# A stream of 64 tiles: one written order for all engines becomes a table with an order for each engine

## The chip, the cores and the metric

The kernel runs on one NeuronCore of a Trainium2 chip. The metric is the device time of one execution in microseconds (us). The engines are TensorE (PE: matrix products and transposes into PSUM), VectorE (DVE), ScalarE (ACT), GpSimd (POOL) and SyncE (SP, which issues the DMAs). Each runs its own instructions strictly in the order in which they are written, and they meet only in semaphores.

## The reference

Four residual blocks over x of shape (4, 512, 128), each on a layer norm of x without affine part:

```python
x = x + attn_a(layernorm(x))     # 16 heads of 8, full softmax
x = x + ffn(layernorm(x))        # two layers: local attention + MLP
x = x + attn_b(layernorm(x))     # linear attention, 16 heads of 8
x = x + ffn(layernorm(x))        # the same two layers, same weights
# one layer of ffn, on h = shift_token(x)
q, k, v = split(h @ wqkv)                    # 8 heads of 64
q, k = rotary_xpos(l2norm(q) * qs, l2norm(k) * ks)
x = x + softmax(mask(8 * q @ k.T)) @ v @ wo  # windows of 64, one back
h = layernorm(shift_token(x)) * lg + lb
a, g = split(h @ w1 + b1)
x = x + (a * gelu(g)) @ w2 + b2
```

All is float32. The change lies in the part that runs both calls of ffn and attn_b between them.

## The kernel before

Attention a comes first, in blocks of its own. Then `stream` runs the rest as one pipeline. A tile is 128 tokens; four tiles are a group (one sequence in one layer); 4 sequences x 2 layers x 2 calls make 16 groups and 64 tiles. `stream_plan` writes one list of (stage, number) pairs, 72 steps long. In step s tile s is projected (`project`: 9 products) and its q and k are rotated on DVE (`rope`: products with cos and sin, L1391 and L1395, then the sums of squares L1402 and the clip L1406); POOL adds the two halves (L971) and multiplies by the reciprocal norms (L976) in the stage `scale`, for which ACT makes the norms (L1279, L1283). Tile s-1 is transposed (`turn`, L1052), copied by ACT (L1258, L1262), scored (`scores`: masks L1065, products L1078) and softened (`soften`: maxima on DVE L1423, exponents on ACT L1272). Tile s-2's exponents are transposed (`turn_p`, L1089) in two halves, of which ACT copies the first (L1290) and DVE the second (L1415), and multiplied with v (`sums`, L1100, then L1430 and L1434 on DVE). Tile s-3's result is transposed (`turn_o`, L1112).

Once in four steps the work of a whole group comes in. I call the steps by it:

| step mod 4 | name here | group work |
|---|---|---|
| 3 | norm step | layer norm before the MLP: `center` (L1153), square (L1311), `var` (L1158), L1317, L1320, L1448, L1452 |
| 0 | w1 step | `w1`: 12 passes of PE (L1165), gelu on ACT between two table loads (L1323, L1328, L1331), three products on DVE (L1468) |
| 1 | w2 step | `w2`: 6 passes (L1173), then L1485 and L1489, or L1478 in the last layer |
| 2 | wo step | `wo`: 8 passes (L1138), Y (L1440), copies on POOL (L991, L993) |

In steps 26 to 41 attention b of each sequence is spread over four further stages: centre, variance and latent (wo step), keys (norm step: L1189, L1509, L1516), context, tokens and features (w1 step: L1196, L1206, L1533 to L1540, L1213), projection, centre and variance (w2 step: L1218, L1546, L1153, L1158, L1457, L1460).

Every engine walks the same list and picks the stages in which it has work, so a stage's place in the list is its place on every engine. PSUM has 8 banks, handed out in turn in PE's order; a product waits until the user of the bank eight places earlier has freed it (`take`).

Of the kernel before, what the change touches and what calls it, by code (L numbers as in the profile page):

```python
# [14 lines left out]
P = 128  # L15
# [701 lines left out]
def stream_plan():  # L717

    plan, norms, number = [], [], {}

    def tile(k, *stages):
        if 0 <= k < TOTAL:
            plan.extend((stage, k) for stage in stages)

    def group(k, *stages):

        if k % TILES == TILES - 1 and 0 <= k < TOTAL:  # L730
# [24 lines left out]
    def var(k, use):
        if k % TILES == TILES - 1 and 0 <= k < TOTAL:
            m = k // TILES
            if use == "mlp" or last_layer(m) and not last_call(m):
                plan.append(("var", number[use, m if use == "mlp" else m % SEQS]))

    for step in range(TOTAL + 8):
        tile(step, "project", "rope")
        group(step - 6, "w2")
        center(step - 7, "b")
        tile(step - 3, "turn_o")
        center(step - 4, "mlp")
        group(step - 5, "w1")
        sequence(step - 9, "context")
        sequence(step - 10, "project_b")
        tile(step - 1, "turn")  # L770
        group(step - 3, "wo")
# [18 lines left out]
    return plan, norms, number  # L790


def stream(nc, a, g, out):

    psum, X, Y, eps, cst, cstb = g.psum, g.X, g.Y, g.eps, g.cst, g.cstb
    plan, norms, number = stream_plan()

    order = []
    for stage, i in plan:
        if stage == "project":  # L800
            order += [("q", i), ("k", i), ("v", i)]
# [37 lines left out]
    with ExitStack() as ctx:  # L839
# [76 lines left out]
        with block:  # L916
            @block.sync
            def _(sp):
# [5 lines left out]
                for stage, k in plan:  # L924
                    if stage == "turn":
# [19 lines left out]
            def _(pool):  # L945
# [21 lines left out]
                for stage, i in plan:  # L967
# [41 lines left out]
                    elif stage == "var" and norms[i][0] == "y":  # L1009
                        n = norms[i][1]  # L1010
                        pool.wait_ge(s("ln_used"), i + 1)
                        low_part(n, "again_shifted", 2 * n)

            @block.tensor
            def _(pe):
# [68 lines left out]
                def turn_p(k):  # L1084
                    for u in (2 * k, 2 * k + 1):
                        pe.wait_ge(s("exped"), u + 1)
                        dst = take("turn_p", u)
                        for c in range(PAIRS):
                            last = nc.tensor.transpose(dst[:, P * c:P * c + P], PW[:, u % 4, c, :], g.ident)  # L1089
                        last.then_inc(s("turned_p"), 1)  # L1090
# [27 lines left out]
                for stage, i in plan:  # L1118
# [6 lines left out]
                    elif stage == "turn_p":  # L1125
                        turn_p(i)
# [14 lines left out]
                    elif stage == "center":  # L1141
                        use, j = norms[i]
# [426 lines left out]
```

## Time and profile before

| what | us |
|---|---|
| time, median of 3 runs (1241.07 to 1248.66) | 1245.42 |
| time of the profiled execution | 1247.89 |
| its span, first to last instruction | 1246.1 |
| PE busy, of the span | 998.1 (80%) |
| DVE busy | 798.1 (64%) |
| ACT busy | 703.9 (56%) |
| POOL busy | 390.8 (31%) |
| mean granted TensorE clock, share of full speed | 0.922 |

The profiled execution's own time is 1.8 us above its span and 2.5 us above the median of the runs. The stream begins some 390 us into the span. Busy time of PE is modelled at the ends of products, so the text goes by the starts of the rows. A group in the forms below is named by its line in the kernel, its engine, and what it writes from what it reads.

### The profile page before, as it was taken

Reading aid. Unit: us, or ns where it says so; the run is one execution under the profiler, and the core shown is the slowest. Engines: PE = TensorE matmul, PEld = TensorE weight load, DVE = VectorE, ACT = ScalarE, POOL = GpSimd, SP = SyncE. Lnnn points to the kernel's source line nnn. Section 1 sums busy time; section 2 is a strip of 40 time slices with the busy share of each in tenths; the row PEclk is TensorE's granted clock in tenths of the full one; section 3 lists DMA queues with packets and bytes.
Section 4 is the critical chain, followed back from the end, with each engine's and each line's share of the span. In section 5 each row is a group of like instructions: output and inputs, shape, how many; then the busy total and the mean of one; then the engine's idle time right before and its main releaser. Section 6 shows DMA issues by size and latency. Waiting matters only on the chain.

```text
span 1246.1 us, 22091 instructions
## 1 busy us (share of the span) xinstructions
PE 998.1 (80%) x8250; PEld 602.5 (48%) x8272; DVE 798.1 (64%) x1381; ACT 703.9 (56%) x1500; POOL 390.8 (31%) x251
## 2 busy tenths in 40 slices
PE   4079986069985788889889898989898898898886
PEld 2023333013323666666556665656565665666652
DVE  4088825058825668678677685867677786676751
ACT  3037763017773567557566565656666576576662
POOL 5000015000003553534444434342434435344330
PEclk9589998569997799999899999999999999999998
DMA  2950001950002211011010010000001010101100
GB/s 65 129 100 9 1 1 38 113 70 2 1 2 51 57 23 22 19 22 23 18 24 14 18 23 18 14 18 14 18 14 23 19 23 19 23 14 35 31 10 17
DMA packets 38268, 36.01 MB, mean 29 GB/s; under 512 B 11478, under 2 KB 30224, under 8 KB 38160
## 3 DMA queue, kind: packets, MB, share of 16 engines
q1 hardware_dynamic: 34708, 31.46, 13.8%
q10 hardware_dynamic: 3456, 3.15, 1.2%
q8 instruction: 67, 1.10, 0.4%
q14 instruction: 37, 0.30, 0.1%
HBM read 15.41 MB, written 4.21 MB: 16 GB/s over the span
## 4 chain that ended last, share of the span: by engine, by line
PE 28%; DVE 13%; POOL 11%; ACT 9%; issue 6%; POOLq 0%; DVEq 0%; ACTq 0%
PE psum L1165 6%; PE psum L1138 5%; POOL f_A L976 4%; POOL f_A L971 4%; ACT f_PW L1272 4%; PE psum L1052 3%; PE psum L1078 2%; PE psum L1089 2%; DVE f_A L1391 2%; DVE f_BS L1395 2%; POOL f_HL L963 2%; DVE f_NM L1423 2%; DVE f_SS L1402 2%; PE psum L1100 2%; PE psum L1158 1%
## 5 line engine op out<-in xcount | busy, mean ns | idle before, releaser
L1272 ACT ACTIVATE f_PW<-psum,f_NM 128x128 f32<-128x128 f32 x512 | 139.3, 383 | 127.9 <-DVE f_NM L1423 127.9
L500 DVE TENSOR_REDUCE a_M<-psum 128x1 f32<-128x512 f32 x256 | 160.2, 684 | 67.5 <-remote 38.7
L976 POOL TENSOR_TENSOR f_A<-f_A,f_RN 128x1024 f32<-128x1024 f32 x64 | 121.7, 1902 | 252.3 <-ACT f_RN L1283 250.0
L971 POOL TENSOR_TENSOR f_A<-f_A,f_BS 128x1024 f32<-128x1024 f32 x64 | 151.6, 2368 | 46.5 <-DVE f_BS L1395 45.0
L430 PE MATMUL psum<-a_KS,a_QS 128*128 128x512 bf16 x238 | 96.7, 413 | 79.7 <-DMA a_KS<-minus_ones 75.9
L547 ACT ACTIVATE a_PT<-psum 128x1024 f32<-128x1024 f32 x128 | 126.4, 1018 | 56.5 <-PE psum L452 56.1
L1391 DVE TENSOR_TENSOR f_A<-psum,cos 128x512 f32<-128x512 f32 x128 | 87.9, 686 | 93.5 <-ACT f_SQ L1240 93.5
L1052 PE MATMUL psum<-const,f_A 128*128 128x128 f32 x512 | 76.8, 299 | 49.6 <-POOL f_A L976 49.6
L452 PE MATMUL psum<-a_QS,a_KS 128*128 128x512 bf16 x252 | 94.5, 390 | 14.6 <-DMA a_QS<-a_MROW 10.4
L1423 DVE TENSOR_REDUCE f_NM<-psum 128x4 f32<-128x512 f32 x128 | 82.3, 685 | 36.4 <-PE psum L1078 36.4
L1042 PE MATMUL psum<-f_wqkv_h,f_HH 128*128 128x512 f32 x192 | 86.7, 451 | 23.0 <-DVE Y L1460 13.1
L430 PEld LDWEIGHTS psum<-a_KS,a_QS 128*128 128x128 bf16 x256 | 25.4, 100 | 159.0 <-DMA a_KS<-minus_ones 75.5
L1052 PEld LDWEIGHTS psum<-const,f_A 128*128 128x128 f32 x512 | 64.8, 154 | 73.3 <-POOL f_A L976 62.9
L1165 PE MATMUL psum<-f_mid,f_w 128*128 128x512 f32 (+1 forms) x192 | 89.7, 619 | 2.7 <-DVE f_mid L1452 2.7
L1100 PE MATMUL psum<-f_VS,f_PT 128*64 128x65 f32 x1024 | 73.8, 225 | 17.9 <-DVE f_mid L1448 12.1
L1395 DVE TENSOR_TENSOR f_BS<-psum,sin 128x512 f32<-128x512 f32 x128 | 87.2, 681 | 0.0
L1100 PEld LDWEIGHTS psum<-f_VS,f_PT 128*64 128x64 f32 x1024 | 65.5, 138 | 30.0 <-issue 30.0
L1402 DVE TENSOR_REDUCE f_SS<-f_SQ 128x16 f32<-128x1024 f32 x64 | 77.4, 1210 | 0.0
L1044 PE MATMUL psum<-f_wqkv_h,f_HL 128*128 128x512 f32 x192 | 76.9, 401 | 0.0
L1043 PE MATMUL psum<-f_wqkv_l,f_HH 128*128 128x512 f32 x192 | 76.9, 400 | 0.0
L1100 PE MATMUL psum<-f_V,f_PT 128*64 128x65 f32 x1024 | 74.1, 226 | 0.0
L1240 ACT ACTIVATE f_SQ<-psum 128x512 f32<-128x512 f32 x128 | 68.5, 585 | 7.6 <-PE psum L1044 7.6
(173 smaller groups left out, 1966.5 us busy)
## 6 DMA issues: line engine op xcount, KB each, us to landing
f_VS<-f_V SPq DMA_DIRECT2D x112, 130.0 KB, 2.3
parts<-a_PRT ACTq DMA_DIRECT2D x24, 128.0 KB, 2.4
a_QS<-parts SPq DMA_DIRECT2D x8, 256.0 KB
a_KS<-parts SPq DMA_DIRECT2D x8, 256.0 KB
a_QS<-parts SPq DMA_DIRECT2D x4, 384.0 KB
a_KS<-parts SPq DMA_DIRECT2D x4, 384.0 KB
raw<-L_ffn_wqkv_dram SPq DMA_DIRECT2D x2, 768.0 KB, 7.0
a_XT<-L_attn_a_x_dram SPq DMA_DIRECT2D x4, 256.0 KB, 4.0
```

The source lines that it names most:

```text
L430: nc.tensor.matmul(psum[:, take("tile", 8 * unit + k), :], QS[:, n, h + k // 4, P * qt:P * qt + P], KS[:, n, h + k // 4, :], start=True, s ...
L500: nc.vector.tensor_reduce(M[:, u % 4, k // 4, k % 4:k % 4 + 1], psum[:, bank("tile", i), :], AX_X, ALU.max)\
L547: nc.scalar.activation(PT[:, head % 8, 2 * (half % 2):2 * (half % 2) + 2, :], psum[:, SLOT[i % 2][0]:SLOT[i % 2][1] + 1, :], ACT.Exp, scal ...
L971: nc.gpsimd.tensor_tensor(A[:, k % 2, :, :], A[:, k % 2, :, :], BS[:, k % 2, :, :], ALU.add)\
L976: nc.gpsimd.tensor_tensor(x, x, RN[:, k % 2, :, None].to_broadcast([P, 2 * HW, DW]), ALU.mult)\
L1052: last = nc.tensor.transpose(dst[:, P * c:P * c + P], A[:, k % 2, w, P * c:P * c + P], g.ident)
L1100: last = nc.tensor.matmul(dst[WIN * w:WIN * w + WIN, c, :], PT[:, u % 4, c, WIN * w:WIN * w + WIN], values[:, k % 4, 2 * c + j, :], start= ...
L1165: nc.tensor.matmul(take(kind, 3 * i + blk)[0:w, :], w1[:, layer, first + lo:first + lo + w], mid[:, :], start=True, stop=True).then_inc(s( ...
L1272: last = nc.scalar.activation(PW[:, u % 4, c, :], psum[:, bank("scores", u), P * c:P * c + P], ACT.Exp, bias=NM[:, u % 4, c:c + 1])
L1391: nc.vector.tensor_tensor(A[:, k % 2, w, :].rearrange("p (h d) -> p h d", d=DW), x.rearrange("p (h d) -> p h d", d=DW), g.cos[:, layer, t, ...
L1395: nc.vector.tensor_tensor(BS[:, k % 2, w, :].rearrange("p (h s d) -> p h s d", s=2, d=DW // 2), x.rearrange("p (h s d) -> p h s d", s=2, d ...
L1423: nc.vector.tensor_reduce(NM[:, u % 4, :], psum[:, bank("scores", u), :].rearrange("p (c x) -> p c x", c=PAIRS), AX_X, ALU.max, negate=Tru ...
```

## The change

`stream_plan` goes. A table `STEP` gives for each engine its own list of stages with their lags, and `engine_plan(engine)` unrolls one engine's list. Banks are still handed out in PE's order. Some stages are cut in two: `project` on ACT into `squares` and `values`, `scale` on ACT becomes `norm`, `turn_p` on PE into two halves, `w1` on DVE into two blocks and the last one (`w1_last`), `center` and `var` into one for each of the three norms. No instruction is added or taken away, and no buffer changes.

```diff
-def stream_plan():
...
-    for step in range(TOTAL + 8):
-        tile(step, "project", "rope")
-        group(step - 6, "w2")
-        center(step - 7, "b")
-        tile(step - 3, "turn_o")
-        center(step - 4, "mlp")
-        group(step - 5, "w1")
-        sequence(step - 9, "context")
-        sequence(step - 10, "project_b")
-        tile(step - 1, "turn")
-        group(step - 3, "wo")
-        tile(step - 2, "turn_p")
-        var(step - 4, "mlp")
-        var(step - 7, "b")
-        center(step - 10, "y")
-        sequence(step - 8, "keys_b")
-        sequence(step - 9, "tokens_b")
...
-        tile(step - 1, "scores")
-        tile(step - 1, "soften")
-        tile(step, "scale")
-        tile(step - 2, "sums")
-        var(step - 10, "y")
-        sequence(step - 7, "latent")
-        sequence(step - 9, "features_b")
+STEP = {
+    "PE": [("project", 0, of_tile), ("turn", 1, of_tile), ("context", 9, of_sequence), ("project_b", 10, of_sequence),
+           ("turn_o", 3, of_tile), ("w1", 5, of_group), ("turn_p", 2, of_tile),
...
+           ("keys_b", 8, of_sequence), ("tokens_b", 9, of_sequence), ("scores", 1, of_tile),
...
+           ("turn_p_2", 2, of_tile), ("latent", 7, of_sequence), ("features_b", 9, of_sequence),
+           ("w2", 6, of_group), ("wo", 3, of_group), ("sums", 2, of_tile), ("store", 6, of_end)],
...
+def engine_plan(engine):
+    plan = []
     for step in range(TOTAL + 8):
...
+        for stage, lag, whose in STEP[engine]:
+            k = step - lag
+            if 0 <= k < TOTAL and whose(k) is not None:
+                if stage == "lead" and not 1 <= k < SEQS or stage == "split" and k >= 3:
+                    continue
+                plan.append((stage, whose(k)))
+    return plan
...
-                for stage, i in plan:
-                    if stage == "project":
+                for stage, i in engine_plan("ACT"):
+                    if stage == "squares":
```

On ACT, from step 50 into step 51 (f_QT and f_KT are the copies of the transposed q and k, f_PW the exponents, f_LN and f_RN the norms, f_SQ the squares, f_V the values), there stood from one copy of q on:

```order
709 L1258 ACTIVATE f_QT<-psum 128x512
710 L1262 ACTIVATE f_KT<-psum 128x4x128
711 L1290 ACTIVATE f_PT<-psum 128x512
712 L1272 ACTIVATE f_PW<-psum,f_NM 128x128 x8
713 L1279 ACTIVATE f_LN<-f_SS 128x16
714 L1283 ACTIVATE f_RN<-f_LN 128x16
715 L1240 ACTIVATE f_SQ<-psum 128x512 x2
716 L1249 ACTIVATE f_V<-psum 128x8x64
```

and stands now:

```order
707 L1257 ACTIVATE f_QT<-psum 128x512
708 L1261 ACTIVATE f_KT<-psum 128x4x128
709 L1248 ACTIVATE f_V<-psum 128x8x64
710 L1298 ACTIVATE f_OT<-psum 128x4x128
711 L1289 ACTIVATE f_PT<-psum 128x512
712 L1278 ACTIVATE f_LN<-f_SS 128x16
713 L1282 ACTIVATE f_RN<-f_LN 128x16
714 L1271 ACTIVATE f_PW<-psum,f_NM 128x128 x8
```

The norms of a tile have moved from behind the exponents of the tile before it to ahead of them; the copies of values stand behind those of q and k.

On DVE, in step 49, a w2 step (f_SS is the clip, f_HH and Y the sum of the MLP, f_PT the copy of the second half of the transposed exponents, f_NM the maxima), there stood:

```order
823 L1406 TENSOR_TENSOR f_SS<-f_SS,tiny 128x16
824 L1485 SCALAR_TENSOR_TENSOR f_HH<-psum,f_vecs,Y 64x512
825 L1485 SCALAR_TENSOR_TENSOR f_HH<-psum,f_vecs,Y 64x511
826 L1489 SCALAR_TENSOR_TENSOR Y<-psum,f_vecs,Y 128x512
827 L1415 COPY f_PT<-psum 128x512
828 L1423 TENSOR_REDUCE f_NM<-psum 128x4 x2
829 L1430 RECIPROCAL f_RD<-psum 128x4
```

and stands now:

```order
823 L1407 TENSOR_TENSOR f_SS<-f_SS,tiny 128x16
824 L1424 TENSOR_REDUCE f_NM<-psum 128x4 x2
825 L1416 COPY f_PT<-psum 128x512
826 L1488 SCALAR_TENSOR_TENSOR f_HH<-psum,f_vecs,Y 64x512
827 L1488 SCALAR_TENSOR_TENSOR f_HH<-psum,f_vecs,Y 64x511
828 L1492 SCALAR_TENSOR_TENSOR Y<-psum,f_vecs,Y 128x512
829 L1431 RECIPROCAL f_RD<-psum 128x4
```

The maxima have moved up, and the copy f_PT stands behind them instead of ahead.

On PE, in step 42 (the first wo step behind attention b), behind the projections, there stood `turn_o`, `turn`, `wo`:

```order
1890 L1112 MATMUL psum<-const,f_ON 128x128 x4
1891 L1052 MATMUL psum<-const,f_A 128x128 x8
1892 L1138 MATMUL psum<-f_OT,f_wo 128x512 x4
```

and behind those `turn_p` and the scores. Now there stands:

```order
1930 L1047 MATMUL psum<-const,f_A 128x128 x8
1931 L1106 MATMUL psum<-const,f_ON 128x128 x4
1932 L1083 MATMUL psum<-const,f_PW 128x128 x4
1933 L1060 MATMUL psum<-constb 64x512 x4
1934 L1073 MATMUL psum<-f_KT,f_QT 64x128 x16
1935 L1083 MATMUL psum<-const,f_PW 128x128 x4
1936 L1134 MATMUL psum<-f_OT,f_wo 128x512 x4
1937 L1094 MATMUL psum<-f_VS,f_PT 64x65
```

`wo` has moved behind the scores, and the second half of `turn_p` too, just ahead of the sums that read its copy.

## Rows read from the trace of the kernel before

**Rows 1.** Page, part 5: the squares (busy, mean ns of one)

```profile
L1240 ACT ACTIVATE f_SQ<-psum 128x512 f32<-128x512 f32 x128 | 68.5, 585 | 7.6 <-PE psum L1044 7.6
```

**Rows 2.** Waits: engine and line, whom for: us in total, times, longest

```profile
POOL f_A L976 <- ACT f_RN L1283: 250.0, 48, 8.3
```

**Rows 3.** Timeline of steps 53 and 54: start, length, instruction, [idle before]

```profile
1072.93 0.18 DVE L1406 TENSOR_TENSOR f_SS<-f_SS,tiny 128x16 f32<-128x16 f32 x1
...
1076.57 2.17 ACT L1272 ACTIVATE f_PW<-psum,f_NM 128x128 f32<-128x128 f32 x8 [2.71 <-DVE f_NM L1423]
...
1080.45 1.90 POOL L976 TENSOR_TENSOR f_A<-f_A,f_RN 128x1024 f32<-128x1024 f32 x1
...
1082.41 1.97 PE L1052 MATMUL psum<-const,f_A 128*128 128x128 f32 x8 [3.02 <-POOL f_A L976]
```

**Rows 4.** Windows: stretch, length, busy time by engine, granted clock (PEclk)

```profile
1082.30:1083.80 1.50, 1.39 (x7) 1.40 (x8) 1.17 (x2) 0.24 (x1) 0.05 (x1) 0.50 0.41 93
...
1052.90:1056.00 3.10, 3.06 (x41) 2.68 (x42) 2.64 (x7) 2.05 (x9) 0.00 (x0) 1.00 0.00 0
```

**Rows 5.** Timeline of PE, steps 51 to 55

```profile
1043.44 0.50 PE L1042 MATMUL psum<-f_wqkv_h,f_HH 128*128 128x512 f32 x1
...
1048.72 1.04 PE L1089 MATMUL psum<-const,f_PW 128*128 128x128 f32 x8
1049.60 1.02 PE L1158 MATMUL psum<-f_ln_squared,const 128*128 128x512 f32 x2
...
1050.79 1.04 PE L1078 MATMUL psum<-f_KT,f_QT 64*64 64x128 f32 x32
...
1054.02 0.50 PE L1042 MATMUL psum<-f_wqkv_h,f_HH 128*128 128x512 f32 x1
...
1056.65 3.60 PE L1165 MATMUL psum<-f_mid,f_w 128*128 128x512 f32 x8
...
1066.39 0.50 PE L1042 MATMUL psum<-f_wqkv_h,f_HH 128*128 128x512 f32 x1
...
1076.61 0.50 PE L1042 MATMUL psum<-f_wqkv_h,f_HH 128*128 128x512 f32 x1
...
1090.36 0.27 PE L1100 MATMUL psum<-f_VS,f_PT 128*64 128x65 f32 x1
...
1091.45 0.50 PE L1042 MATMUL psum<-f_wqkv_h,f_HH 128*128 128x512 f32 x1
...
1093.63 0.60 PE L1112 MATMUL psum<-const,f_ON 128*128 128x128 f32 x4
```

**Rows 6.** Timeline of DVE, step 55

```profile
1094.36 0.69 DVE L1391 TENSOR_TENSOR f_A<-psum,cos 128x512 f32<-128x512 f32 x1 [1.45 <-ACT f_SQ L1240]
...
1098.00 1.32 DVE L1406 TENSOR_TENSOR f_SS<-f_SS,tiny 128x16 f32<-128x16 f32 x1
...
1099.24 0.68 DVE L1415 COPY f_PT<-psum 128x512 f32<-128x512 f32 x1
```

**Rows 7.** Line L1402, once for each tile: the whole line, then tiles 11, 26, 42

```profile
L1402 DVE TENSOR_REDUCE f_SS<-f_SQ x64: 1207/1209/1214, 401.4 to 1190.5; 128x16 f32<-128x1024 f32 x64
...
519.87 1.21 DVE L1402 TENSOR_REDUCE f_SS<-f_SQ 128x16 f32<-128x1024 f32 x1
699.01 1.21 DVE L1402 TENSOR_REDUCE f_SS<-f_SQ 128x16 f32<-128x1024 f32 x1
940.46 1.21 DVE L1402 TENSOR_REDUCE f_SS<-f_SQ 128x16 f32<-128x1024 f32 x1
```

**Rows 8.** Timeline of DVE in attention b: keys, maxima; tokens

```profile
842.85 0.75 DVE L1509 TENSOR_SCALAR f_NEGK<-psum 128x256 f32<-128x256 f32 x2
...
844.94 1.28 DVE L1423 TENSOR_REDUCE f_NM<-psum 128x4 f32<-128x512 f32 x2
...
856.78 0.19 DVE L1533 TENSOR_SCALAR f_DEN<-psum 128x32 f32<-128x32 f32 x1 [0.27 <-PE psum L1206]
...
858.35 0.42 DVE L1540 TENSOR_TENSOR f_OB<-psum,f_DEN 128x256 f32<-128x256 f32 x1
```

More of the change, by code:

```diff
@@ L803, in stream @@
             order += [("turned_q", i), ("turned_k", i)]
-        elif stage in ("turn_p", "scores", "sums", "keys_b", "tokens_b"):
+        elif stage in ("scores", "sums", "keys_b", "tokens_b"):
             order += [(stage, 2 * i), (stage, 2 * i + 1)]
+        elif stage in ("turn_p", "turn_p_2"):
+            order += [("turn_p", 2 * i + (stage == "turn_p_2"))]
         elif stage == "w1":
@@ L809, in stream @@
             order += [("latent", i), ("query_b", i)]
-        elif stage in ("turn_o", "wo", "center", "var", "w2", "context", "features_b", "project_b", "store"):
+        elif stage[:7] == "center_":
+            order += [("center", number[stage[7:], i])]
+        elif stage[:4] == "var_":
+            order += [("var", number[stage[4:], i])]
+        elif stage in ("turn_o", "wo", "w2", "context", "features_b", "project_b", "store"):
             order += [(stage, i)]
@@ L923, in _ @@
                 sp.wait_ge(s("zeroed"), 3)
-                for stage, k in plan:
-                    if stage == "turn":
+                for stage, k in engine_plan("SP"):
+                    if stage == "values":
                         sp.wait_ge(s("v_copied"), k + 1)
@@ L965, in low_part @@
                         pool.wait_ge(s(done), before + half + 1)
-                for stage, i in plan:
+                for stage, i in engine_plan("POOL"):
                     if stage == "scale":
@@ L1082, in scores, with turn_p @@
                     last.then_inc(s("scores"), 1)
[L1084 to L1090, printed above, removed]
+                def turn_p(u):
+                    pe.wait_ge(s("exped"), u + 1)
+                    dst = take("turn_p", u)
+                    for c in range(PAIRS):
+                        last = nc.tensor.transpose(dst[:, P * c:P * c + P], PW[:, u % 4, c, :], g.ident)
+                    last.then_inc(s("turned_p"), 1)
                 def sums(k):
@@ L1381, in _ @@
                                             ALU.subtract).then_inc(s("lead_shifted"), 1)
-                for stage, i in plan:
+                for stage, i in engine_plan("DVE"):
                     if stage == "rope":
@@ L1409, in _ @@
                         lead(i)
[L1410 removed]
+                    elif stage == "turn_p_2":
                         u = 2 * i + 1
@@ L1441, in _ @@
                           .then_inc(s("y_mid"), 1)
-                    elif stage == "var":
-                        use, j = norms[i]
-                        x = psum[:, bank("center", i), :]
-                        dve.wait_ge(s("ln_recip"), i + 1)
+                    elif stage[:4] == "var_":
+                        use, j = stage[4:], i
+                        at_norm = number[use, j]
+                        x = psum[:, bank("center", at_norm), :]
+                        dve.wait_ge(s("ln_recip"), at_norm + 1)
                         if use == "mlp":
```

131 lines of the change are left out of this document (66 added, 65 removed).

## The prediction, as it stands on record

> **What bounds the kernel now.** I read the page first, then the waits, then the timeline of one group of the stream, engine by engine. Of all engines PE is busiest, but its busy time does not say where it waits. The waits do: the largest in the stream is POOL's before the multiplication by the norms, 250 us in 48 times, and ACT is what it waits for [rows 2]. Rows 3 show the case. The clip of tile 53 is done at 1073.1, so its norms could follow. But ACT's list puts them behind the exponents of tile 52, which end at 1078.7, since those wait for maxima. POOL then still adds the halves and multiplies until 1082.35, and PE, idle for 3.02 us, transposes. Behind the wait PE ran at half its clock (1.2 instead of 2.4 GHz) [rows 4]. So the chain scores, maxima, exponents, norms, multiplication, transposition, copies, scores runs through every step.
>
> How much of a group is waiting I get from PE's own work [rows 5]. A pass over 512 columns takes 0.43 (8 passes of L1165 in 3.60, ends overlapping); projection 2.18 (1091.45 to 1093.63); `turn` or a whole `turn_p` 0.88 (1048.72 to 1049.60), `turn_o` half of it, 0.43; the norm's product with the masks 1.19 (1049.60 to 1050.79), of which I give the product 0.95; masks and scores so 0.24 + 1.0; sums 1.09 (1090.36 to 1091.45). A step without group work is 2.18 + 0.88 + 0.43 + 0.88 + 1.25 + 1.09 = 6.7. With two norm products the norm step is 8.6, with 12 passes the w1 step 11.9, with 6 the w2 step 9.3, with 8 the wo step 10.2: 40.0 a group. The starts of the projections (lines L1042) give 10.6, 12.4, 10.2 and 14.8 for the four, 48.0 in all [rows 5]. So 8 us of each group are waits and low clock, 4.6 of them in the wo step (3.0 wait, 1.6 clock).
>
> **The change, part by part.** No instruction comes or goes, so what counts is what each waits for in the new lists. I set P = 0 where PE starts a step's projection.
>
> *Norms ahead of exponents.* q is projected at P + 1.0, squared 0.6 later [rows 1], so DVE's rotation starts at P + 1.7. From there to the end of the clip it takes 4.96 (1094.36 to 1099.32) [rows 6]: P + 6.7. The two norms on ACT lie within the 1.7 between the exponents' end and the multiplication in rows 3; I take 0.6, as one of the squares, and bound them by 0 and 1.7. POOL multiplies in 1.9 [rows 3]. That gives P + 9.3, with 1.7 P + 10.4. The transposition comes at 2.2 in the next step, so it waits no more if a step has 7.1 or more (8.2 by the upper bound). The 3.02 in the wo step and the smaller waits of this kind go.
>
> *Copy of the second half behind the maxima.* This is the new wait. PE's sums of the second half need DVE's copy, DVE's copy comes behind the maxima, and these behind the clip. In a short step: clip done 6.7, maxima 1.28 [rows 8], copy 0.68 [rows 6], half of the sums 0.55: the next projection cannot start before P + 1.0 + 0.7 + 4.96 + 1.28 + 0.68 + 0.55 and some 0.15 between them = 9.3. This ring replaces the old chain. The norm step becomes 9.3 (work 8.6), the w2 step 9.4 (work 9.3), the wo step 10.5: its work is 10.2, and it starts with DVE 1 us late from Y of the w2 step, so the copy comes at 9.9, just as PE gets to it. In the w1 step the 12 passes lie ahead of the scores: they end at 2.18 + 0.88 + 0.43 + 5.16 + 0.43 + 1.25 + 0.1 = 10.4, and maxima, copy and half the sums bring 10.4 + 1.28 + 0.68 + 0.55 + 0.15 = 13.05, which is 0.65 slower than the 12.4 of before. ACT's gelu, its second table load and its copy of the first half run under the scores there; if the copy were late by its whole length it would cost 0.7 a group. The group: 9.3 + 13.05 + 9.4 + 10.5 = 42.3 against 48.0.
>
> *The clip itself* took 0.18 at 1072.93 and 1.32 at 1098.00; the second time POOL's addition was running and both ended together [rows 3, 6]. In the new order the addition starts 1.1 ahead of it in almost every step, so I take 1.32 always. With 0.18 the ring would be 8.2 and the norm step PE's 8.6. The Trainium skill ("SBUF — State Buffer", section "Who interferes with whom") has a rule for it: a DVE instruction with two SBUF inputs and a GpSimd one that reads SBUF exclude each other, and the one issued first holds the port to its end. By that rule, and the row at 1098.00 agrees, the clip always pays here; without it the group would be about 41.6 and the time some 9 us less.
>
> *Scores inside the layer norm.* In the norm step the scores separate `center` and `var`. ACT's square ends under the scores, so `var` waits for nothing, and the bank wait of the sums for the layer norm's output goes. All of this is inside the 9.3 above.
>
> *Products moved past copies and SP.* SP's moves of v are issued on `values`, still a step and more ahead of the sums. ACT copies v 1.2 later than before. Nothing waits for that. If it did, it would cost at most 1.2 in a step.
>
> *Attention b, 16 steps.* Here the new lists lose. In the w1 step, `features` (PE) needs DVE's tokens, which now stand behind the copy. Context and tokens add 1.0 and 1.0 to PE (I take eight 144-column passes each, from 0.43 for 512), so the scores end at 12.5; maxima and copy bring 14.6, and the tokens take 2.0 (856.78 to 858.77) [rows 8]: 16.7. PE idles from 12.9. Then features 0.4, and the third block of `w1` on DVE frees the sums' bank: 17.4 + 1.1 = 18.5. In the w2 step `center` for y stands ahead of the scores and needs x, which DVE writes behind the clip: 6.7 + 0.75 = 7.5, PE idle 2.7; then center 0.95, scores 1.25, var 0.95, half `turn_p` 0.43, w2 2.6, sums 1.1: 14.8. In the wo step `latent` stands ahead of `wo` and needs Y, for which DVE goes through clip, maxima, copy and Y (6.7 + 1.3 + 0.7 + 0.7 = 9.4, PE idle 2); latent's four passes at most 1.7, wo 3.4, sums 1.1: 15.7. In the norm step the keys put 2.1 between clip and maxima (842.85 to 844.94) [rows 8]: 9.3 + 2.1 = 11.4. Together 60.4 a cycle. Before, 16 such steps took 940.46 - 699.01 = 241.5, 60.4 a cycle [rows 7]. So nothing is won. The waits of 3.6, 2.7 and 2.0 can each let the clock fall at 1.6 a time; bounds 0 and 4.8 a cycle, and I take 1.0.
>
> **The sum**, by stretches between the squares' sums of tiles [rows 7]. Tiles 0 to 11, 118.5 before: in the first two little can change, and I leave them at 16 (118.5 less nine steps of 11.4, a little under the 11.9 a step of tiles 11 to 26); then five steps of 9.3 (with one norm step), 10.5 twice, 13.05, 9.4 make 90: 106, gain 12. Tiles 11 to 26, 179.1: three groups of 42.3 and three steps of 31.8 in all, 158.7, gain 20. Tiles 26 to 42: 241.5 + 4, loss 4. Tiles 42 to 63, 250.0: five groups and a wo step, 222.0, gain 28. The tail: one short chain less ahead of the last `wo`, gain 3. The gain is 59 to 60 of the profiled execution's 1247.9: 1188. The median of the runs stands 2.5 lower, so I forecast **1185**.
>
> **Rivals.**
>
> 1. *As worked out*, 1172 to 1198. For it: every term is a row's start or length, and the waits it removes recur the same in each group. Chance 0.50.
> 2. *Attention b costs more.* If all three waits let the clock fall and `features` is late by more, 5 to 8 us more a cycle and some of the ramp's gain lost: 1198 to 1222. For it: PE idles longer there than in any plain step of before. Against: the waits themselves, 8.3 a cycle, are already in the terms, and 1.0 of clock with them. Chance 0.19.
> 3. *More is won.* If the clip is not held up or the gaps between stages overlap, the plain groups come near 41 and the wo step to PE's 10.2: 1155 to 1172. Against: the clip at 1098.00. Chance 0.16.
> 4. *DVE sets the pace.* Its list (rotation and clip 5.0, maxima 1.3, copy 0.7, sums 1.2) is 8.2 a step, plus 2.3 for w2 and up to 2.2 for w1. If it carries lateness from one step into the next, plain groups need 45 to 46: 1222 to 1239. Against: it adds to 38 of 42.3 a group. Chance 0.05.
> 5. *Slower: low clock in plain steps.* Many short PE waits, between turn_p and sums, could keep the clock at 1.2 GHz where one long wait let it recover. A fall costs 1.6; some 37 falls in the 64 steps eat the gain of 60, and one in each of the 52 plain or ramp steps gives 1185 + 83 = 1268. Against: behind a wait of 1.1 the window at 1052.9 shows full clock [rows 4], and the new plain waits are 0.7 (norm step) and 1.7 (w1 step), nearly none in the other two. The Trainium skill describes this mechanism ("TensorE: Matmul & The Clock Gate", section "A second HAM failure mode: psum-queue depth-cycling"): frequent small idles between groups of products made the clock swing. By that rule the kernel could be slower; the window of rows 4 speaks against it here. Chance 0.05.
> 6. *No change*: the chain simply reforms at the old length, through a bank that exponents free. Exponents end 3.0 after the maxima start, ahead of the next step's transposition by over 2 us, so I see none. 1239 to 1252, chance 0.02. The rest, 0.03, is below 1155.
>
> **Numbers.** A measurement of this kernel tells a change from none beyond about 0.5%, 6 us. Cases 1 to 4 are faster, 0.93; no change 0.02; slower 0.05. The range 1163 to 1216 takes in case 1, most of 2 and half of 3, some 0.8.
>
> **What would show it.** Right, if in a plain group: POOL's multiplication follows its addition within 0.8 us; PE no longer waits for it; the projections start 9.3, 13, 9.4 and 10.5 apart; PE's only waits are in the middle of the sums, for the copy by DVE; and if in attention b PE waits 3 to 4 us for DVE's tokens ahead of `features`. Wrong, if the clip is short in most steps (then faster), if the granted clock in plain groups falls under 0.95, or if the attention b cycle takes over 65 us.

## The result, and the profile after

| | before | after |
|---|---|---|
| median of 4 runs each, us | 1247.04 | 1192.95 |
| lowest to highest | 1241.07 to 1249.16 | 1191.47 to 1193.12 |
| span of the profiled execution | 1246.1 | 1191.1 |
| mean granted clock | 0.922 | 0.925 |

The ratio is 0.9582, 95% interval 0.9532 to 0.9631: 54 us faster. 1185 was forecast, with 1163 to 1216 as the range.

Where POOL waited before its multiplication [rows 2], this is what its waits say now (engine and line, whom for: total, times, longest):

```profile
POOL f_A L966 <- DVE f_BS L1396: 219.2, 58, 10.4
...
POOL f_A L971 <- ACT f_RN L1282: 107.0, 59, 5.4
```

The multiplication (now L971) waits 107 us in place of 250. The 219 in front of the addition L966 is idle time that costs nothing: POOL stands ready before DVE has written its halves. PE's own waits, the same view:

```profile
PE psum L1094 <- DVE f_PT L1416: 18.0, 26, 3.3
...
PE psum L1210 <- DVE f_OB L1543: 13.3, 4, 3.4
...
PE psum L1149 <- DVE X L1549: 7.9, 4, 2.4
PE psum L1175 <- DVE Y L1462: 6.9, 4, 1.7
PE psum L1047 <- POOL f_A L971: 5.4, 4, 3.4
PE psum L1094 <- DVE f_mid L1450: 5.1, 4, 1.3
```

PE waits for the multiplication (L1047, before L1052) only 4 times, all of them in the first steps of the stream; before it was 49.6 us in 27 times. New is the middle of the sums (L1094, behind DVE's copy). The other places that occur four times each lie in attention b: `features` (L1210) and `latent` (L1175), both new, `center` for y (L1149), and the sums that wait for the bank of f_mid. The waits for X and for f_mid were there before too (6.5 us in 4 times, 12.1 us in 11); of those for f_mid the ones in plain groups are gone.

The timeline of a plain group (steps 45 to 48) answers to [rows 3, 5, 6]:

```profile
944.30 0.50 PE L1037 MATMUL psum<-f_wqkv_h,f_HH 128*128 128x512 f32 x1
...
953.78 0.50 PE L1037 MATMUL psum<-f_wqkv_h,f_HH 128*128 128x512 f32 x1
...
958.75 2.36 POOL L966 TENSOR_TENSOR f_A<-f_A,f_BS 128x1024 f32<-128x1024 f32 x1 [1.10 <-DVE f_BS L1396]
...
959.77 1.37 DVE L1407 TENSOR_TENSOR f_SS<-f_SS,tiny 128x16 f32<-128x16 f32 x1
...
961.42 0.21 ACT L1282 ACTIVATE f_RN<-f_LN 128x16 f32<-128x16 f32 x1
...
961.71 1.90 POOL L971 TENSOR_TENSOR f_A<-f_A,f_RN 128x1024 f32<-128x1024 f32 x1 [0.61 <-ACT f_RN L1282]
...
961.78 2.18 ACT L1271 ACTIVATE f_PW<-psum,f_NM 128x128 f32<-128x128 f32 x8
...
964.12 0.50 PE L1037 MATMUL psum<-f_wqkv_h,f_HH 128*128 128x512 f32 x1
...
972.72 0.27 PE L1094 MATMUL psum<-f_VS,f_PT 128*64 128x65 f32 x1 [0.33 <-DVE f_PT L1416]
...
973.33 0.50 PE L1037 MATMUL psum<-f_wqkv_h,f_HH 128*128 128x512 f32 x1
...
985.80 0.27 PE L1094 MATMUL psum<-f_VS,f_PT 128*64 128x65 f32 x1 [0.81 <-DVE f_PT L1416]
986.42 0.50 PE L1037 MATMUL psum<-f_wqkv_h,f_HH 128*128 128x512 f32 x1
```

Clip, norms, multiplication now follow each other, and the exponents begin beside the multiplication, no longer ahead of it. The projections start 9.48 (w2 step), 10.34 (wo step), 9.21 (norm step) and 13.09 (w1 step) apart, 42.12 in all. The windows over this group and over tiles 42 to 63 show the clock at 1.00 (length, busy time of PE, PEld, DVE, ACT and POOL, granted clock, DMA share, GB/s):

```profile
944.30:986.45 42.15, 41.01 (x423) 28.65 (x419) 37.39 (x62) 31.58 (x78) 20.68 (x13) 1.00 0.11 24
...
916.64:1137.40 220.76, 215.21 (x2180) 150.49 (x2173) 191.27 (x317) 164.28 (x398) 109.58 (x71) 1.00 0.12 26
```

It is 1.00 over tiles 11 to 26 too, and 0.95 over tiles 26 to 42. The squares' sums, L1403, one for each tile, answer to [rows 7] (the whole line, then tiles 11, 26, 42):

```profile
L1403 DVE TENSOR_REDUCE f_SS<-f_SQ x64: 1206/1208/1210, 398.6 to 1137.4; 128x16 f32<-128x1024 f32 x64
...
503.31 1.21 DVE L1403 TENSOR_REDUCE f_SS<-f_SQ 128x16 f32<-128x1024 f32 x1
661.46 1.21 DVE L1403 TENSOR_REDUCE f_SS<-f_SQ 128x16 f32<-128x1024 f32 x1
916.64 1.21 DVE L1403 TENSOR_REDUCE f_SS<-f_SQ 128x16 f32<-128x1024 f32 x1
```

| stretch, us | before | forecast | after |
|---|---|---|---|
| tiles 0 to 11 | 118.5 | 106 | 104.7 |
| tiles 11 to 26 | 179.1 | 158.7 | 158.2 |
| tiles 26 to 42, attention b | 241.5 | 245.5 | 255.2 |
| tiles 42 to 63 | 250.0 | 222.0 | 220.7 |
| last tile to the end | 55.6 | 3 less | 53.8 |

Three stretches came within 1.3 us. Attention b lost 13.7 instead of 4. These 9.7 us, less the 3.1 more that the other three won, and 1.2 less at the end, are nearly the whole distance from 1185 to 1193.

### The profile page after: what moved, and what is told of

Read it like the earlier page. It is cut to its first block, busy times and chain, and to the rows that moved or that the text cites. A ratio compares the mean times of both kernels' runs of the same rounds, so it can differ in the third digit from the quotient of the medians.

```text
span 1191.1 us, 22117 instructions
## 1 busy us (share of the span) xinstructions
PE 1000.9 (84%) x8272; PEld 595.0 (50%) x8272; DVE 827.9 (70%) x1381; ACT 718.4 (60%) x1500; POOL 391.0 (33%) x251
## 4 chain that ended last, share of the span: by engine, by line
PE 48%; DVE 11%; issue 3%; ACT 3%; POOL 2%; DVEq 0%; POOLq 0%
PE psum L1162 7%; PE psum L1094 5%; PE psum L1134 5%; PE psum L1037 4%; PE psum L1073 4%; PE psum L1170 3%; PE psum L1047 3%; PE psum L1039 3%; PE psum L1038 3%; PE psum L1083 3%; DVE f_NM L1424 2%; DVE f_A L1392 2%; PE psum L1106 2%; DVE f_BS L1396 2%; DVE f_SS L1403 2%
## 5 line engine op out<-in xcount | busy, mean ns | idle before, releaser
L966 POOL TENSOR_TENSOR f_A<-f_A,f_BS 128x1024 f32<-128x1024 f32 x64 | 151.0, 2359 | 219.5 <-DVE f_BS L1396 219.2
L430 PE MATMUL psum<-a_KS,a_QS 128*128 128x512 bf16 x256 | 104.9, 419 | 76.1 <-DMA a_KS<-minus_ones 73.8
L971 POOL TENSOR_TENSOR f_A<-f_A,f_RN 128x1024 f32<-128x1024 f32 x64 | 121.9, 1904 | 107.7 <-ACT f_RN L1282 107.0
L1271 ACT ACTIVATE f_PW<-psum,f_NM 128x128 f32<-128x128 f32 x512 | 138.9, 382 | 14.0 <-DVE f_NM L1424 10.9
L1237 ACT ACTIVATE f_SQ<-psum 128x512 f32<-128x512 f32 x128 | 75.9, 609 | 84.2 <-PE psum L1039 79.6
L1094 PE MATMUL psum<-f_VS,f_PT 128*64 128x65 f32 x1024 | 81.8, 230 | 23.5 <-DVE f_PT L1416 18.0
L1094 PEld LDWEIGHTS psum<-f_VS,f_PT 128*64 128x64 f32 x1024 | 68.8, 141 | 56.4 <-issue 29.3
L1094 PE MATMUL psum<-f_V,f_PT 128*64 128x65 f32 x1024 | 82.1, 230 | 0.0
L1407 DVE TENSOR_TENSOR f_SS<-f_SS,tiny 128x16 f32<-128x16 f32 x64 | 80.3, 1255 | 2.2
L1083 PE MATMUL psum<-const,f_PW 128*128 128x128 f32 x512 | 79.0, 277 | 0.0
L1403 DVE TENSOR_REDUCE f_SS<-f_SQ 128x16 f32<-128x1024 f32 x64 | 77.3, 1208 | 0.0
```

The source lines that it names most:

```text
L430: nc.tensor.matmul(psum[:, take("tile", 8 * unit + k), :], QS[:, n, h + k // 4, P * qt:P * qt + P], KS[:, n, h + k // 4, :], start=True, s ...
L966: nc.gpsimd.tensor_tensor(A[:, k % 2, :, :], A[:, k % 2, :, :], BS[:, k % 2, :, :], ALU.add)\
L971: nc.gpsimd.tensor_tensor(x, x, RN[:, k % 2, :, None].to_broadcast([P, 2 * HW, DW]), ALU.mult)\
L1094: last = nc.tensor.matmul(dst[WIN * w:WIN * w + WIN, c, :], PT[:, u % 4, c, WIN * w:WIN * w + WIN], values[:, k % 4, 2 * c + j, :], start= ...
L1271: last = nc.scalar.activation(PW[:, u % 4, c, :], psum[:, bank("scores", u), P * c:P * c + P], ACT.Exp, bias=NM[:, u % 4, c:c + 1])
```

## The experiments

All kernels change only the lists of stages, except where the clip is named. The stretches in the table are measured between the squares' sums on DVE, from one profiled execution each; the 390 us or so ahead of the stream differ by up to 6 us from run to run, so a stretch says more than a median. The profiled executions lie within 5 us of their medians, but that of x17_wo_both lies 7.9 above. A single step comes out otherwise by the squares' sums than by the starts of PE's projections, where an order moves DVE against PE; the text says which it uses. The groups of after, x1, x2 and x4 are alike to 0.6 us; those of before differ among themselves, 46.6 to 49.6, and so do those of x5 and x9. Each ratio is taken against the runs of the kernel before that were made beside it (medians 1245.3 to 1247.3). The four columns behind the ratio are: tiles 0 to 11; a plain group; an attention b cycle (a quarter of tiles 26 to 42); tiles 42 to 63.

| kernel | median | ratio [95%] | 0-11 | group | cycle | 42-63 |
|---|---|---|---|---|---|---|
| before | 1247.04 | 1 | 118.5 | 48.0 | 60.4 | 250.0 |
| after | 1192.95 | 0.9582 [0.9532, 0.9631] | 104.7 | 42.1 | 63.8 | 220.7 |
| x5_old_norm | 1237.97 | 0.9927 [0.9894, 0.9959] | 117.6 | 47.8 | 60.3 | 246.8 |
| x9_old_scale | 1271.98 | 1.0215 [1.0173, 1.0258] | 118.5 | 49.5 | 62.1 | 260.0 |
| x6_old_norm_scale | 1220.43 | 0.9788 [0.9741, 0.9836] | 117.9 | 44.8 | 61.0 | 236.6 |
| x17_wo_both | 1216.37 | 0.9755 [0.9716, 0.9795] | 115.0 | 45.1 | 61.7 | 237.4 |
| x1_norms_back | 1226.70 | 0.9843 [0.9795, 0.9891] | 109.9 | 44.5 | 63.8 | 232.7 |
| x2_copy_first | 1182.99 | 0.9482 [0.9432, 0.9531] | 103.3 | 41.7 | 62.7 | 218.7 |
| x4_no_clip | 1177.63 | 0.9450 [0.9405, 0.9496] | 100.9 | 42.0 | 61.3 | 220.1 |
| x3_attention_b | 1158.53 | 0.9285 [0.9210, 0.9360] | 105.8 | 42.1 | 54.7 | 220.8 |
| x11_b_keys | 1176.39 | 0.9447 [0.9410, 0.9483] | 104.7 | 42.1 | 59.8 | 220.7 |
| x20_b_keys_both | 1166.21 | 0.9337 [0.9273, 0.9400] | 105.9 | 42.1 | 57.5 | 220.8 |
| x10_b_copy | 1155.99 | 0.9271 [0.9227, 0.9315] | 102.8 | 41.7 | 56.4 | 218.7 |
| x8_b_clip_copy | 1150.23 | 0.9226 [0.9177, 0.9275] | 99.5 | 41.7 | 56.0 | 218.6 |

**Which move brings the gain: one stage put back.** x1_norms_back, against the changed kernel:

```
"ACT": ... ("keys_b", 8, of_sequence),
-      ("norm", 0, of_tile),
       ("var_mlp", 4, of_group), ("var_b", 7, of_sequence), ("var_y", 10, of_sequence),
       ("soften", 1, of_tile),
+      ("norm", 0, of_tile),
```

> The changed kernel with one stage of one engine put back: ACT takes `norm` behind `soften` again. Theory (the norms ahead of the exponents are the main gain): the chain exponents, norms, multiplication, transposition comes back with a wait of 0.6 to 1.7 us a step on POOL and PE, a plain group takes about 44.6 us instead of 42.15, and the whole 1215 to 1240, most likely 1226. Rival (PE's own new order is the gain, with wo behind the scores and fewer bank waits): 1200 or less.

1226.7, group 44.5: the theory's numbers, and 34 us of the 54 hang on this one stage. By PE's starts the w1 step takes 14.9 instead of 13.1 and the w2 step 10.1 instead of 9.5; the other two steps stay. Its waits:

```profile
POOL f_A L973 <- ACT f_RN L1284: 321.2, 61, 10.0
...
PE psum L1049 <- POOL f_A L973: 33.2, 31, 3.9
```

PE waits for the multiplication 31 times for 33.2 us, where the changed kernel has 4 times and 5.4. That it is still 20 us faster than before (interval 0.9795 to 0.9891) shows that the other moves carry a share too.

**The same move alone, from the other side.** x5_old_norm, against the order before:

```
"ACT": ... ("split", SEQS, of_tile),
+      ("norm", 0, of_tile),
       ("soften", 1, of_tile),
-      ("norm", 0, of_tile),
```

> All engines in the order of the kernel before, with one stage of one engine moved: ACT takes `norm` ahead of `soften`. Theory (POOL's list, which has w2 and wo ahead of scale, and PE's, which has wo ahead of the scores, still hold the multiplication back): 1236 to 1247, hardly a change. Rival (ACT's order alone is the gain): about 1200 or less.

1238.0: 9 us, inside the theory's range. The timeline (ACT, POOL and PE, from the end of a w2 step into the wo step) says why:

```profile
1021.05 0.22 ACT L1284 ACTIVATE f_RN<-f_LN 128x16 f32<-128x16 f32 x1
...
1022.12 2.44 POOL L960 TENSOR_TENSOR f_HL<-Y,f_HH 64x512 fp32r<-64x512 f32 x2 [8.02 <-DVE Y L1494]
...
1027.15 1.90 POOL L973 TENSOR_TENSOR f_A<-f_A,f_RN 128x1024 f32<-128x1024 f32 x1
...
1029.11 1.82 PE L1049 MATMUL psum<-const,f_A 128*128 128x128 f32 x8 [2.99 <-POOL f_A L973]
```

The norms are done at 1021.3, but POOL's list has `w2` (f_HL) ahead of `scale`, and stands 8.02 us in it for Y. PE waits its 2.99 as before [rows 3].

x9_old_scale makes the other half alone:

```
-"POOL": [w2, wo, lead, split, scale, var_y, latent]
+"POOL": [lead, split, scale, w2, wo, var_y, latent]
```

> All engines in the order of the kernel before, with one stage of one engine moved: POOL takes its scale stage ahead of w2 and wo. Theory (the norms on ACT, behind the exponents, still come last in every step, so POOL's addition alone is early, 1.3 a wo step): 1230 to 1238. Rival (POOL's queue was the larger of the two hindrances, since x5_old_norm, ACT's alone, gave only 9): 1222 or less.

1272.0, 2.1% slower than before: a miss for both. POOL now waits in `scale` for norms that stand behind the exponents, and what is queued behind it is late:

```profile
1011.43 1.90 POOL L973 TENSOR_TENSOR f_A<-f_A,f_RN 128x1024 f32<-128x1024 f32 x1 [5.26 <-ACT f_RN L1284]
...
1014.69 1.10 PE L1151 MATMUL psum<-f_mid,const 128*128 128x512 f32 x2 [2.88 <-POOL f_mid L990]
```

The 5.26 push f_mid back, and PE waits 2.88 for it. Over the whole run PE waits 21 us less for the multiplication than before (28.2 in 16 times), but 34 more for f_mid of POOL (35.7 in 14 times, before 2.2 in one) and 8 more for a bank that Y of `w2` frees (13.4 in 7 times, before 5.4); half clock behind some of these waits is part of what is left of the 27. I had priced only what the earlier addition saves, not who is queued behind the wait.

x6_old_norm_scale makes both moves (the diffs of x5_old_norm and x9_old_scale):

> As x5_old_norm, and POOL takes its scale stage ahead of w2 and wo; PE, DVE and SP keep the order of the kernel before. Theory (these two moves take away the 3.0 us wait and the 1.6 us of half clock behind it in each wo step, which is 4.6 of the 8 us that a plain group has in waits; attention b's 16 steps stay at 60.4 a cycle instead of 63.8): 1175 to 1195. Rival (PE's new order is needed too, because the sums and wo wait for banks): 1215 or more.

1220.4, group 44.8: the rival. One move gives -9, the other +27, both together -26. By the squares' sums the wo step fell as expected, from 14.9 to 10.8, and the w1 step from 12.2 to 11.6, but the norm step rose from 10.7 to 11.2 and the step w2 from 10.4 to 11.2. The waits of PE from 1000 to 1090 show where the rest went:

```profile
PE psum L1096 <- DVE Y L1494: 3.1, 2, 1.6
PE psum L1096 <- DVE f_mid L1452: 2.9, 2, 1.5
```

3.0 us a group at the sums, for banks that DVE frees late. In the changed kernel these two waits are gone from the plain groups, and the group is 2.7 shorter; it differs from x6_old_norm_scale in PE's and DVE's order and in the places of the other stages on ACT. I tried one stage, x17_wo_both:

```
 "PE":  ... turn,
-        wo,
         turn_p, ... store, scores,
+        wo,
         sums, ...
 "DVE": ... project_b,
-        wo,
         turn_p_2, ... lead, soften,
+        wo,
         sums, ...
```

> As x6_old_norm_scale, and the wo stage stands behind the scores on PE and behind the maxima on DVE, as in the changed kernel; the other stages of PE and DVE keep the order of the kernel before. Theory (the 3.0 us a plain group that x6_old_norm_scale still waits at the sums are for banks that DVE frees with the layer norm's f_mid and with Y of w2, and wo's place touches neither): the wo step falls from 10.8 to 10.3 at best, the whole 1210 to 1222. Rival (wo's place is what PE's new order gives): the group falls from 44.8 to about 42.5, the whole 1190 to 1198.

1216.4, group 45.1: as the theory has it. wo's place alone is worth nothing beyond the scatter of the runs. Which other stages of the new order give the 2.7 was not isolated.

**The ring of clip, maxima and copy.** x4_no_clip:

```
 act.wait_ge(s("summed_squares"), k + 1)          # was "clipped"
-nc.scalar.activation(LN, SS, ACT.Ln)
+nc.scalar.activation(LN, SS, ACT.Ln, bias=g.tiny[:, 0:1])
-nc.vector.tensor_tensor(SS, SS, g.tiny, ALU.max).then_inc(s("clipped"), 1)
```

> The changed kernel without DVE's clip: ACT takes the logarithm of the sums plus 1e-24 instead of the sums clipped at 1e-24, so only sums near zero would come out otherwise. Theory (the clip lies in the ring and is held for the length of POOL's addition): 1.1 us less in the norm step's ring, norm step 8.7, w1 step unchanged at 13.05 or up to 1 less if its scores are not PE's bound, w2 and wo steps 0.1 to 0.3 less, three of the four steps of attention b 1.1 less; together 20 to 25 us, the whole 1168 to 1175. Rival (the clip is off the path, its time is only DVE's): 1190 to 1196.

1177.6, 15 us faster than the changed kernel where 18 to 25 were expected, and not where I looked for it. The plain group stays, 42.0 for 42.1. Steps 1 to 3, without group work, fell from 9.1, 9.7 and 9.2 to 7.4, 7.8 and 7.9, but step 0 rose from 6.1 to 7.4: DVE's casts there (L1372) no longer stand behind the clip but beside POOL's two operations, and take 3.80 for 0.85. The attention b cycle fell from 63.8 to 61.3, all but a little of it in the w2 step. The timeline of a plain norm step without the clip:

```profile
953.50 1.29 DVE L1423 TENSOR_REDUCE f_NM<-psum 128x4 f32<-128x512 f32 x2 [0.93 <-PE psum L1075]
...
955.70 0.27 PE L1096 MATMUL psum<-f_VS,f_PT 128*64 128x65 f32 x1 [0.17 <-DVE f_PT L1415]
```

DVE is early and waits 0.93 for the scores, which stand behind `center`. The sums' wait falls from 0.33 to 0.17, no more, and the w1 step keeps its 0.81. So the ring through the clip binds where PE has little to do; in plain groups PE's own work does.

x2_copy_first:

```
 "PE":  ... turn_p,
+        turn_p_2,
         center_mlp, ... var_y,
-        turn_p_2,
         latent, ...
 "DVE": ... keys_b,
+        turn_p_2,
         soften,
-        turn_p_2,
         tokens_b, ...
```

> The changed kernel with the whole of turn_p together on PE (first and second half in one place, ahead of the scores) and DVE's copy of the second half ahead of the maxima. Theory (the ring clip, maxima, copy, second half of the sums paces norm and w1 steps): w1 step 12.0 instead of 13.1 and norm step 8.7 instead of 9.3, but DVE and ACT then pace part of the w2 and wo steps; a plain group 40.4 to 42.0, the whole 1180 to 1188. Rival (the ring does not bind): 1190 to 1196. Second rival (DVE's list becomes the bound): slower than 1196.

1183.0, inside the theory's range, group 41.7. By PE's starts the w1 step falls from 13.1 to 11.9 and the norm step from 9.2 to 8.7, the theory's two numbers (12.0 and 8.7), and PE waits in neither (the norm step, 999.63 to 1008.31):

```profile
999.63:1008.31 8.68, 8.68 (x106) 6.41 (x102) 7.62 (x12) 5.72 (x12) 4.75 (x5) 1.00 0.14 33
```

So this wait was indeed the ring's. But the w2 step goes from 9.5 to 10.3 and the wo step from 10.3 to 10.9, which gives back 1.3 of the 1.7. In the wo step the masks, to which PE now comes earlier, wait for a bank that the rotation frees:

```profile
993.71 0.41 PE L1062 MATMUL psum<-constb 64*64 64x512 bf16 x4 [0.45 <-DVE f_BS L1398]
```

**Attention b.** x3_attention_b:

```
 "PE":  project_b ahead of project; latent behind wo
 "DVE": project_b ahead of rope; w1_last right behind w1;
        tokens_b ahead of soften; latent behind wo
```

> The changed kernel with its order for attention b's 16 steps altered: on PE project_b ahead of project and latent behind wo; on DVE project_b ahead of rope, the last block of w1 right behind w1, tokens_b ahead of soften, latent behind wo. Plain groups are as they were. Theory (the three waits of attention b, at features, center of y and latent, and the half clock behind them, are only an effect of where these stages stand): the cycle falls from 63.8 to about 53 (w1 step 15.2, w2 step 12.1, wo step 13.6, norm step 12.1), the granted clock there is 1.00, and the whole takes 1142 to 1158. Rival (bank waits or the clock persist, so that a cycle keeps 60 us or more): 1175 or more.

1158.5, just past the theory's 1142 to 1158, and far from the rival's 1175. The cycle was to be 53. It is 54.4 in these windows (w1, w2, wo and norm step), of which PE is busy 51.8, with the clock at 1.00 throughout:

```profile
742.00:758.90 16.90, 15.57 (x133) 10.73 (x132) 12.84 (x25) 11.52 (x24) 4.25 (x2) 1.00 0.04 9
758.90:770.20 11.30, 11.30 (x109) 7.55 (x108) 10.53 (x19) 8.21 (x21) 6.65 (x4) 1.00 0.11 25
770.20:784.30 14.10, 14.10 (x114) 8.27 (x113) 10.56 (x18) 9.43 (x23) 8.12 (x7) 1.00 0.09 20
784.30:796.40 12.10, 10.84 (x111) 8.03 (x110) 10.53 (x21) 9.35 (x25) 4.25 (x2) 1.00 0.11 23
```

So the three waits of attention b, and the half clock behind them, came only from where these stages stand. What was short of 53 is the w1 step, 15.2 expected and 16.6 by PE's starts: PE waits 0.52 in the sums for DVE's copy and 0.81 at `project_b`, the first stage of its next list, for ACT's copy. The norm step keeps 1.26 of wait. I went for the norm step's 1.3 with x11_b_keys (on DVE, `keys_b` from ahead of `tokens_b` to behind `turn_p_2`):

> The order of x3_attention_b with one stage more moved: on DVE keys_b stands behind the copy of the second half, not ahead of the maxima. Theory (in the norm step the keys hold up maxima, copy and the layer norm's f_mid, which frees the sums' bank; PE waits 1.26 there): the norm step of attention b falls from 12.1 to 11.2, the others stay, the whole 1151 to 1157. Rival (the next step's context then waits for the keys): 1159 or more.

1176.4, 18 slower than x3_attention_b. The rival has the number, but neither has the mechanism. ACT and PE in the norm step:

```profile
740.86 0.38 ACT L1352 ACTIVATE f_VB<-psum 128x256 f32<-128x256 f32 x1 [4.60 <-DVE f_NEGK L1514]
...
744.65 0.24 PE L1096 MATMUL psum<-f_VS,f_PT 128*64 128x65 f32 x1 [4.26 <-DVE f_mid L1452]
```

ACT's own list still has `keys_b` ahead of the norms and of the layer norm's second half. So ACT stands 4.60 for DVE's f_NEGK, f_mid comes late, and PE waits 4.26 for its bank where it waited 1.26. In all four cycles PE then starts the next step at half clock; by PE's starts the norm step takes 15.1 to 15.5 instead of 12.1, and the w1 step behind it 17.6 to 19.0 instead of 16.6. x20_b_keys_both moves it on ACT as well (behind `soften`; on DVE behind `var_y`):

> The order of x3_attention_b with keys_b moved on both engines that take part in it: on ACT behind the exponents, on DVE behind the layer norms' second halves (x11_b_keys had moved it on DVE alone, and ACT, which kept it ahead of the norms, stood 4.6 us in wait for it). Theory (a stage can go later if all its engines move it): the norm step of attention b falls from 12.1 to 11.0 to 11.4, the next step stays at 16.9, the whole 1150 to 1157. Rival (keys this late hold up the context or the sums of the next step): 1160 or more.

1166.2. The runs of the two kernels overlap (1160 to 1171, 1148 to 1163), but the cycle, 57.5 for 54.7, is longer too: the rival, and a bank is the mechanism. PE's timeline:

```profile
742.52 0.24 PE L1096 MATMUL psum<-f_VS,f_PT 128*64 128x65 f32 x1 [1.27 <-DVE f_mid L1452]
...
744.84 0.77 PE L1039 MATMUL psum<-f_wqkv_h,f_HH 128*128 128x512 f32 x1 [1.64 <-DVE f_KB L1521]
```

The wait that I wanted away is still there, 1.27. With the keys out of its way DVE stands 1.52 for the scores instead, which lie behind the keys' products on PE, so the keys in between had held up nobody. And the next projection waits 1.64 for the bank that the keys are read from; in three of the four cycles it starts at half clock.

**Together.** x10_b_copy joins x3_attention_b and x2_copy_first, x8_b_clip_copy leaves out the clip as well:

> The order of x3_attention_b with that of x2_copy_first on top, the clip as in the changed kernel; the computation is the reference's. Theory (PE's own work, 41.2 a plain group, is the floor there, and the copy's place is worth 0.45 a group; in attention b it is worth nothing): 1148 to 1156. Rival (the mask's wait for DVE's rotation, 0.45 in each step of x2_copy_first, falls into attention b too): 1157 to 1165.

> The order of x3_attention_b with that of x2_copy_first on top, and no clip (ACT takes the logarithm of the sums plus 1e-24, as in x4_no_clip). Theory (three separate gains that add up: 34 from attention b's order, 4 in the first steps and up to 10 in attention b from the clip, 0.5 to 0.9 a plain group from the copy, since DVE has 4.7 us a group less to do): 1136 to 1146. Rival (they overlap, since x3 already removes the waits in attention b that the clip lengthens): 1147 to 1153.

x10_b_copy, 1156.0, is level with x3_attention_b: the copy's place wins 3.0 in tiles 0 to 11, some 2.1 in each of the other plain stretches, and loses 6.8 in attention b, which I had at nothing. By PE's starts the w1 step goes there from 16.6 to 17.6 in every cycle; PE now waits 2.15 for ACT's f_OF at `project_b`. And behind this wait the clock fell in two of the four cycles (the w2 steps of tiles 29 and 41). Shown are tile 33, where it held, and tile 41:

```profile
754.96:766.49 11.53, 11.53 (x109) 7.60 (x107) 9.57 (x14) 8.16 (x20) 4.26 (x2) 1.00 0.11 25
...
865.37:878.49 13.12, 13.12 (x110) 8.68 (x108) 9.69 (x14) 8.05 (x20) 4.27 (x2) 0.87 0.10 22
```

x8_b_clip_copy, 1150.2, is the rival's case: leaving out the clip is worth 3.3 at the start. The 1.6 in attention b is one fall of the clock less, one cycle in four; every other step there is as long as in x10_b_copy. Both beat the changed kernel, by 37 and 43 us; x8_b_clip_copy is the fastest, x10_b_copy the fastest with the computation unchanged, if only by what the intervals can't separate from x3_attention_b.

## Why the prediction was right, step by step

**The chain broke as forecast.** POOL stands 0.61 us between its addition and its multiplication (0.8 was the bound), PE waits for it no more in plain groups, the wo step went from 14.8 to 10.34 by PE's starts. x1_norms_back confirms the stage, x5_old_norm and x9_old_scale that it takes both lists.

**Step times right, one reason wrong.** Forecast 9.3, 13.05, 9.4, 10.5 and 42.3 a group; measured 9.21, 13.09, 9.48, 10.34 and 42.12. The ring is there: x2_copy_first takes it away and both its waits go. But it was to set the norm step with 0.7 of wait, and the trace shows 0.33; in the w1 step it shows 0.81, where 1.15 were to be lost. PE's own work was undersized instead: 42.12 less these waits is 41.0 a group, not 40.0. x4_no_clip agrees, with a group that moves by 0.15 only where 0.7 was forecast. Two errors of 1 us each met, so that the group came out to 0.2 us is in part luck.

**The clip** was sized rightly and placed wrongly. It took 1.37 at 959.77, with POOL's addition begun at 958.75, and both ended at 961.1. The Trainium skill ("SBUF — State Buffer", "Who interferes with whom") says that the order of issue decides who blocks; the trace agrees in 61 of the 64 tiles, and in the three others, tiles 4 to 6, no POOL operation had begun first and the clip took 0.17. But its 9 us were to come from the plain groups, where x4_no_clip found 0.15 each. Of the 15 us that it did find, 10 lie in attention b and 4 in tiles 0 to 11.

**Attention b is the mis-sized term:** +4 forecast, +13.7 measured. The waits stood where they were put: `features` 3.3 to 3.4 (forecast 3.6), `center` for y 1.7 to 2.4 (2.7), `latent` 1.73 (2.0). What was short is the clock. I took 1.0 a cycle for it. These rows and this window show a fall behind `features` that lasts into a w2 step, and a second one behind `center`:

```profile
765.79 0.66 PE L1210 MATMUL psum<-const,f_OB 128*128 128x128 f32 x4 [3.37 <-DVE f_OB L1543]
...
768.51 0.63 PE L1038 MATMUL psum<-f_wqkv_l,f_HH 128*128 128x512 f32 x1
...
775.97 1.12 PE L1149 MATMUL psum<-X,const 128*128 128x512 f32 x2 [1.86 <-DVE X L1549]
...
777.27 1.75 PE L1073 MATMUL psum<-f_KT,f_QT 64*64 64x128 f32 x32
...
778.95 2.06 PE L1155 MATMUL psum<-f_ln_squared,const 128*128 128x512 f32 x2
```

```profile
768.00:770.30 2.30, 2.30 (x6) 1.82 (x7) 0.61 (x2) 0.60 (x1) 0.00 (x0) 0.50 0.00 0
...
777.30:779.00 1.70, 1.70 (x37) 1.37 (x29) 0.00 (x0) 1.24 (x4) 0.35 (x1) 0.54 0.00 0
```

A pass of the projection takes 0.43 from start to start here, 0.23 at full clock, and the projection 3.43 in place of 2.18: 1.2. Behind the wait of 1.86 the scores take 1.75 for 1.04 and `var` 2.06 for 1.13: 1.6. The two don't simply add, since a slow projection leaves less to wait at `center`. What they cost together is the length of the step. In x1_norms_back, with the same lists but for one stage, there is a cycle in which neither wait was followed by a fall; its w2 step takes 14.78, the forecast's 14.8, with a wait of 2.40 at `center`:

```profile
783.81:798.59 14.78, 12.38 (x112) 7.86 (x109) 10.89 (x17) 8.16 (x20) 2.50 (x2) 1.00 0.09 19
```

In the changed kernel the same step takes 17.05, 17.12 and 17.11 by PE's starts where both fell, and 15.49 in the one cycle where only the first did. The w1 step takes 18.49 to 19.30 for a forecast of 18.5, the longest where the clock fell early. Against 14.78 and 18.49 the clock costs 2.2 a cycle instead of 1.0. The norm step adds 0.7: there the sums' second half waits 1.27 for a bank (L1094 behind f_mid), which I had not seen. The wo step adds 0.2. Together these are 2.1 of the 2.4 a cycle, 9.7 in four, that were missing; the rest is that the stretch was measured on DVE, and by PE's starts takes 254.1, not 255.2. x4_no_clip, in which PE waits 0.56 to 1.07 for X and the clock holds behind it, has a w2 step of 14.0 to 14.1, and x3_attention_b shows the same stages with neither these waits nor low clock.

**Rivals.** Case 1 came (1172 to 1198). Low clock in plain steps didn't: tiles 42 to 63 show 1.00. The swing that the Trainium skill describes ("TensorE: Matmul & The Clock Gate", "A second HAM failure mode: psum-queue depth-cycling") is not to be seen behind the plain waits of 0.33 and 0.81, but the clock did fall in attention b, behind waits of 3.3 and of 1.9 to 2.4. DVE, busy 37.4 of the 42.15 of the group's window, did not set the pace.

## What to carry to other kernels

Where every engine has a list of its own, a chain that crosses engines is broken only if each of them has the stage early: one half of such a pair alone gave -9 us, the other +27, both -26. For each stage that is moved ask who is queued behind it on that engine, and which bank it holds; both keys experiments lost by these. Check that a dependence ring is longer than the engines' own work before pricing a cut in it: the clip lay in the ring and was worth 0.15 us a group where PE was full, 1.3 to 1.9 a step in the three steps without group work. And measure steps on the engine for which they were forecast: by DVE's squares' sums the norm step of x2_copy_first seems 0.4 longer, by PE's starts it is 0.5 shorter.

## What the runs showed of the hardware

The clock is not told by a wait's length alone. In x10_b_copy PE stood 2.15 at `project_b` in each of four cycles, at the same place of the same order. Behind two of these waits the granted clock fell, and the w2 step took 13.1; behind the other two it stayed at 1.00, and the step took 11.5. So one fall cost 1.6 there. In the changed kernel the clock fell at each of the four waits of 3.3 to 3.4 for `features`; in x1_norms_back one of 3.37 passed without a fall:

```profile
781.99 0.66 PE L1212 MATMUL psum<-const,f_OB 128*128 128x128 f32 x4 [3.37 <-DVE f_OB L1545]
```

No run here shows what decides it.

The clip, 128 by 16 elements, took either 0.17 to 0.18 us or as long as a POOL operation held it. In the changed kernel a POOL operation had begun ahead of it in 61 tiles, and in each of them the clip ended 0.03 us after that operation, up to 1.66 us after its own start. In the kernel before this was so in 36 tiles; in the other 28, with no POOL operation begun ahead of it, it took 0.17 to 0.18.
